# ScalarE instead of POOL makes the reciprocal deviation and shift of a layernorm, in a one-core macaron block with a selective scan

## The reference, cut to what matters

```python
def _layernorm(x, axis=-1, eps=1e-05):
    m = jnp.mean(x, axis=axis, keepdims=True)
    v = jnp.var(x, axis=axis, keepdims=True)
    return (x - m) / jnp.sqrt(v + eps)
...
    x = x + 0.5 * _L0_ffn_ref(_layernorm(x, axis=-1), L0_ffn_Ws, ...)
    x = x + _L0_attn_ref(_layernorm(x, axis=-1), ...)
    x = x + 0.5 * _L0_ffn_ref(_layernorm(x, axis=-1), L0_ffn_Ws, ...)
```

## Time and profile before

| what | value |
|---|---|
| median of 3 runs | 4454.32 us (4450.94 to 4455.48) |
| the profiled execution | 4447.92 us, span 4446.2 us |
| PE busy, mean granted clock | 3866.4 us (87%), 0.955 |
| DVE busy | 3971.1 us (89%) |
| ACT busy | 3327.9 us (75%) |
| POOL busy | 3950.6 us (89%) |
| DMA | 434.67 MB, mean 98 GB/s |
| chain that ended last, shares of the span | PE 39%, DVE 24%, issue 15%, POOL 12%, ACT 9% |

### The profile page before, as it was taken

How to read it: one execution, slowest core, us unless ns; L and a number is a source line. 1 busy time by engine, 2 the same in 40 slices (tenths; PEclk the granted TensorE clock), 3 DMA queues, 4 the chain that set the end, 5 groups by cost and what they waited for, 6 DMA issues and landing times.

```text
span 4446.2 us, 50132 instructions
## 1 busy us (share of the span) xinstructions
PE 3866.4 (87%) x12736; PEld 1277.6 (29%) x12736; DVE 3971.1 (89%) x5441; ACT 3327.9 (75%) x4991; POOL 3950.6 (89%) x1740
## 2 busy tenths in 40 slices
PE   6786877999999999999999999999999999678868
PEld 2221222232323323332232333223232323122223
DVE  2669999999999999999999999999999999999963
ACT  4567777877878787877878787887878777677744
POOL 0559999999999999999999999999999999999950
PEclk9898888999999999999999999999999999799979
DMA  2234554445444543444454445444544454434410
GB/s 77 60 81 99 115 117 97 96 108 117 94 98 112 112 96 92 116 108 102 96 116 100 97 101 122 96 102 103 117 94 95 113 116 94 112 95 111 94 34 5
DMA packets 151917, 434.67 MB, mean 98 GB/s; under 512 B 16402, under 2 KB 50451, under 8 KB 151124
## 3 DMA queue, kind: packets, MB, share of 16 engines
q1 hardware_dynamic: 151636, 431.46, 41.9%
HBM read 150.38 MB, written 12.58 MB: 37 GB/s over the span
## 4 chain that ended last, share of the span: by engine, by line
PE 39%; DVE 24%; issue 15%; POOL 12%; ACT 9%; DMA 1%; SPq 0%; DVEq 0%; ACTq 0%; POOLq 0%
DVE work L778 10%; POOL work L962 6%; PE d_ps L487 6%; POOL work L953 5%; PE s_ps L534 4%; DVE dA_ps L778 4%; PE y_ps L449 4%; PE b_ps L480 4%; PE a_ps L466 4%; DVE work L783 3%; PE a_ps L480 3%; PE s_ps L567 2%; DVE sg_sb L858 2%; PE b_ps L466 2%; ACT L637 2%
## 5 line engine op out<-in xcount | busy, mean ns | idle before, releaser
L962 POOL TENSOR_TENSOR work<-dd_sb,bc_sb 128x2048 f32<-128x2048 f32 x512 | 2327.9, 4547 | 49.3 <-DMA dd_sb<-dd_src 49.3
L609 ACT ACTIVATE dA_ps<-dd_sb,a_sb 128x512 f32<-128x512 f32 x2048 | 1367.3, 684 | 554.6 <-DVE work L783 290.1
L953 POOL TENSOR_TENSOR work<-work,bc_sb 128x1024 f32<-128x1024 f32 x640 | 1511.3, 2368 | 46.9 <-DVE work L778 46.5
L778 DVE TENSOR_TENSOR_SCAN work<-dA_ps,work 128x512 f32<-128x512 f32 x1280 | 1495.0, 1205 | 51.8 <-POOL work L962 41.4
L778 DVE TENSOR_TENSOR_SCAN dA_ps<-dA_ps,work 128x512 f32<-128x512 f32 x768 | 935.0, 1217 | 6.3 <-ACT dA_ps L609 4.8
L487 PE MATMUL d_ps<-sg_sb,wd_sb 128*128 128x512 f32 x1408 | 648.4, 593 | 4.8 <-DVE sg_sb L858 4.8
L449 PE MATMUL y_ps<-work,sel_sum 128*32 128x512 f32 x4096 | 578.2, 636 | 83.2 <-POOL work L953 56.3
L783 DVE TENSOR_TENSOR work<-dA_ps,bc_sb 128x512 f32<-128x512 f32 x768 | 523.2, 681 | 8.1
L466 PE MATMUL a_ps<-xT_sb,wg_sb 128*128 128x512 f32 x768 | 427.9, 640 | 113.0 <-ACT sg_sb L637 103.1
L466 PE MATMUL b_ps<-xT_sb,wg_sb 128*128 128x512 f32 x640 | 358.3, 642 | 59.0 <-DVE xs_sb L851 55.2
L637 ACT ACT_TABLE_LOAD x256 | 328.4, 1283 | 70.7 <-PE d_ps L487 66.5
(11 more groups left out here) (122 smaller groups left out, 4059.1 us busy)
## 6 DMA issues: line engine op xcount, KB each, us to landing
dd_sb<-dd_src SPq DMA_DIRECT2D x512, 512.0 KB, 8.5
bc_sb<-bc_rows SPq DMA_DIRECT2D x256, 512.0 KB, 5.3
xr_sb<-in_L_attn_x SPq DMA_DIRECT2D x16, 256.0 KB, 3.1
x<-xr_sb SPq DMA_DIRECT2D x16, 256.0 KB, 6.9
bc_rows<-dbc_sb SPq DMA_DIRECT2D x128, 32.0 KB, 1.7
xr_sb<-x SPq DMA_DIRECT2D x16, 256.0 KB, 2.9
out<-xr_sb SPq DMA_DIRECT2D x16, 256.0 KB, 6.9
wg_sb<-in_L_ffn_Wg SPq DMA_DIRECT2D x1, 1408.0 KB, 7.1
```

The source lines that it names most:

```text
L609: act.activation(dA_ps[:, g % NDA, :], dd_sb[:, b, c, 0, :], ACT.Exp, scale=a_sb[:, l, b, j, c:c + 1]).then_inc(dA_ready, 1)
L778: dve.tensor_tensor_scan(dA if on_dve(i) else tile, dA, tile, 0.0, ALU.mult, ALU.add).then_inc(scanned, 1)
L953: pool.tensor_tensor(work[:, g % RING], work[:, g % RING], bc_sb[:, j, 0, :].unsqueeze(1).broadcast_to([128, 2, T]), ALU.mult).then_inc(po ...
L962: pool.tensor_tensor(work[:, g % RING:g % RING + 2].rearrange("p h c t -> p (h c) t"), dd_sb[:, b, :, 1, :], bc_sb[:, j, 1, :].unsqueeze(1 ...
```

## The change

The four small POOL instructions of a norm go. In their place ACT runs seven: logarithm of the variance plus epsilon and the negated mean (`log_act`), exponential of -0.5 times the logarithm (`rstd_act`), and for each of the four row blocks the negated mean times that (`shift_act`). `bn_sb`, `mv_sb` and `rs_sb` get two halves that norms use in turn, so that DVE waits for the norm before the last (`nb_ready`, m - 1) and not for the last one. The unused `neg_half` and its memset on DVE go (`VPREP` 9 to 8), and so do `end_pool` and the POOL semaphores. PE's wait for the expert weights follows its table. All tables of numbers are set anew; two of them are shown.

```diff
-CORE = {"exp": -10, "scan": -1, "dbu": -12, "dve_prod": 1, "pool_prod": 12, "sum": 30, "y0": 88, "y1": 8}
+CORE = {"exp": -9, "scan": -1, "dbu": -34, "dve_prod": 2, "pool_prod": -15, "sum": 24, "y0": 87, "y1": 8}
-END = {"yt": 27, "xo": 33, "bn": 47, "nb": 60, "xtok": 67, "ht": 89, "h": 76, "store": 90, "acc": 4}
+END = {"yt": 19, "xo": 35, "bn": 36, "ln": 38, "rs": 47, "nb": 51, "xtok": 59, "ht": 77, "h": 77, "store": 90, "acc": 2}
...
-        bn_sb = sb("bn_sb", [128, TB, 6])
-        mv_sb = sb("mv_sb", [128, TB, 2])
-        rs_sb = sb("rs_sb", [128, 4, TB])
+        bn_sb = sb("bn_sb", [128, 2, TB, 6])
+        mv_sb = sb("mv_sb", [128, 2, TB, 2])
+        rs_sb = sb("rs_sb", [128, 2, 3, TB])
...
-                if t == FFN[0][0]:
+                if t == FFN[0][0] + min(0, *FFN_AT.values()):
                     pe.wait_ge(w_ffn, 16 * FFN_LOADS)
...
-                                          scale=rs_sb[:, 0, k:k + 1], bias=rs_sb[:, 2, k:k + 1])
+                                          scale=rs_sb[:, m % 2, 0, k:k + 1], bias=rs_sb[:, m % 2, 2, k:k + 1])
...
+            def log_act(what, f):
+                m = NORM_OF[what, f]
+                act.wait_ge(mv_done, m + 1)
+                if m > 1:
+                    act.wait_ge(xtok_ready, m - 1)
+                act.activation(rs_sb[:, m % 2, 0, :], mv_sb[:, m % 2, :, 1], ACT.Ln, bias=eps_sb[:, 0:1])
+                act.activation(rs_sb[:, m % 2, 1, :], mv_sb[:, m % 2, :, 0], ACT.Copy, scale=-1.0).then_inc(var_log, 1)
+
+            def rstd_act(what, f):
+                m = NORM_OF[what, f]
+                act.wait_ge(var_log, m + 1)
+                act.activation(rs_sb[:, m % 2, 0, :], rs_sb[:, m % 2, 0, :], ACT.Exp, scale=-0.5).then_inc(rstd_done, 1)
+
+            def shift_act(what, f):
+                m = NORM_OF[what, f]
+                act.wait_ge(rstd_done, m + 1)
+                for k in range(TB):
+                    last = act.activation(rs_sb[:, m % 2, 2, k:k + 1], rs_sb[:, m % 2, 1, k:k + 1], ACT.Copy,
+                                          scale=rs_sb[:, m % 2, 0, k:k + 1])
+                last.then_inc(nb_ready, 1)
...
-                if m > 0:
-                    dve.wait_ge(shift_done, m)
+                if m > 1:
+                    dve.wait_ge(nb_ready, m - 1)
...
-            def norm_pool(what, f):
-                m = NORM_OF[what, f]
-                pool.wait_ge(mv_done, m + 1)
-                if m > 0:
-                    pool.wait_ge(xtok_ready, m)
-                pool.tensor_scalar(rs_sb[:, 3, :], mv_sb[:, :, 1], EPS, None, ALU.add).then_inc(ve_done, 1)
-                pool.wait_ge(ve_done, m + 1)
-                pool.tensor_tensor(rs_sb[:, 0, :], rs_sb[:, 3, :], neg_half[:, :], ALU.pow).then_inc(rstd_done, 1)
-                pool.wait_ge(rstd_done, m + 1)
-                pool.tensor_tensor(rs_sb[:, 1, :], mv_sb[:, :, 0], rs_sb[:, 0, :], ALU.mult).then_inc(shift_done, 1)
-                pool.wait_ge(shift_done, m + 1)
-                pool.tensor_scalar(rs_sb[:, 2, :], rs_sb[:, 1, :], -1.0, None, ALU.mult).then_inc(nb_ready, 1)
```

More of the change, by code:

```diff
@@ L31 @@
 W, PERIOD = 128, 32
-CORE = {"exp": -10, "scan": -1, "dbu": -12, "dve_prod": 1, "pool_prod": 12, "sum": 30, "y0": 88, "y1": 8}
-PREP = {"dc1": 83, "dc0": 60, "sq": -20, "ms": -6, "rms": -10, "xn": -4, "xp0": 17, "conv0": 16, "xp1": 25, "conv1": 23,
-        "silu_xc": 27, "z0": 105, "zc0": 97, "z1": 114, "zc1": 106, "silu_z": 123, "wx": 46, "dbc": 38, "rows": 32, "dt0": 48,
-        "sp0": 52, "delta0": 57, "du0": 60, "dt1": 77, "sp1": 71, "delta1": 76, "du1": 79, "dd0": 63, "dd1": 135, "bc": 98}
@@ new lines @@
+PREP = {"dc1": 84, "dc0": 62, "sq": -14, "ms": -19, "rms": -6, "xn": -4, "xp0": 9, "conv0": 18, "xp1": 13, "conv1": 23,
+        "silu_xc": 27, "z0": 94, "zc0": 97, "z1": 106, "zc1": 105, "silu_z": 123, "wx": 29, "dbc": 46, "rows": 78, "dt0": 41,
+        "sp0": 49, "delta0": 61, "du0": 65, "dt1": 63, "sp1": 70, "delta1": 77, "du1": 79, "dd0": 56, "dd1": 178, "bc": 123}
+NEAR = {"dc1": 95, "dc0": 80, "sq": 16, "ms": 13, "rms": 24, "xn": 30, "xp0": 40, "conv0": 49, "xp1": 44, "conv1": 56,
+        "silu_xc": 59, "z0": 99, "zc0": 101, "z1": 105, "zc1": 108, "silu_z": 123, "wx": 65, "dbc": 60, "rows": 73, "dt0": 69,
+        "sp0": 73, "delta0": 81, "du0": 81, "dt1": 83, "sp1": 90, "delta1": 91, "du1": 92, "dd0": 86, "dd1": 174, "bc": 103}
@@ new lines @@
+POST = {"x1": 49, "wblk": 83, "h": 90, "attn": 90, "x2": 98}
+POST_NEAR = {"x1": -81, "wblk": 9, "h": 14, "attn": 20, "x2": 55}
+FFN_AT = {"gb": -2, "xs": 4, "g0": -8, "g1": 3, "g2": 5, "burst": 5, "u0": 7, "u1": 7, "u2": 18, "hh0": 13, "hh1": 14,
+          "hh2": 23, "down": 21}
+START = {"load": -96, "bn": -56, "ln": -52, "rs": -49, "nb": -46, "xtok": -45, "xt": -42, "xT": -40, "lg": -41, "lg_sb": -34, "mx": -32,
+         "mi": -30, "gap": -56, "we": -31, "eq": -24, "den": -56, "inv": -26, "comb": -49, "ct": -15, "gates": -20}
@@ L340, in build @@
         APREP = 2 + 2 * NL + NL * NBLK
-        VPREP, PPREP = 9, 10
+        VPREP, PPREP = 8, 10
         ps_of = {"a": a_ps, "b": b_ps}
@@ L648, in norm_act @@
                     last = act.activation(xtok[:, k, :], xr_sb[:, x_slot(FFN[f][1], n), k, :], ACT.Identity,
-                                          scale=rs_sb[:, 0, k:k + 1], bias=rs_sb[:, 2, k:k + 1])
+                                          scale=rs_sb[:, m % 2, 0, k:k + 1], bias=rs_sb[:, m % 2, 2, k:k + 1])
                 last.then_inc(xtok_ready, 1)
-            def start_act(t):
+            def log_act(what, f):
[16 more added lines that the diff above has]
+                last.then_inc(nb_ready, 1)
+            def start_act(t):
+                if (f := UNIT_OF.get(t - START["ln"])) is not None:
+                    log_act("start", f)
+                if (f := UNIT_OF.get(t - START["rs"])) is not None:
+                    rstd_act("start", f)
+                if (f := UNIT_OF.get(t - START["nb"])) is not None:
+                    shift_act("start", f)
                 if (f := UNIT_OF.get(t - START["xtok"])) is not None:
@@ L669, in end_act @@
             def end_act(t):
+                if (f := UNIT_OF.get(t - E * PERIOD - END["ln"])) is not None and FFN[f][1] == 1:
+                    log_act("ln2", f)
+                if (f := UNIT_OF.get(t - E * PERIOD - END["rs"])) is not None and FFN[f][1] == 1:
+                    rstd_act("ln2", f)
+                if (f := UNIT_OF.get(t - E * PERIOD - END["nb"])) is not None and FFN[f][1] == 1:
+                    shift_act("ln2", f)
                 if (f := UNIT_OF.get(t - E * PERIOD - END["acc"])) is not None:
@@ L865, in norm_dve @@
                 for k in range(TB):
-                    last = dve.bn_stats(bn_sb[:, k, :], xr_sb[:, x_slot(FFN[f][1], n), k, :])
+                    last = dve.bn_stats(bn_sb[:, m % 2, k, :], xr_sb[:, x_slot(FFN[f][1], n), k, :])
                 last.then_inc(bn_done, 1)
                 dve.wait_ge(bn_done, m + 1)
-                if m > 0:
-                    dve.wait_ge(shift_done, m)
+                if m > 1:
+                    dve.wait_ge(nb_ready, m - 1)
                 for k in range(TB):
-                    last = dve.bn_aggr(mv_sb[:, k, :], bn_sb[:, k, :])
+                    last = dve.bn_aggr(mv_sb[:, m % 2, k, :], bn_sb[:, m % 2, k, :])
                 last.then_inc(mv_done, 1)
@@ L1036, in _ @@
                 start_pool(t)
-                end_pool(t)
 def laid_out(name, a):
```

13 lines of the change are left out of this document (3 added, 10 removed).

## The result

The changed kernel takes 4473.37 us (median of 6 runs, 4470.05 to 4475.26), the kernel before 4452.63 us beside it (6 runs, 4446.46 to 4455.48). The ratio is 1.0048, 95% interval 1.0036 to 1.0061: **slower by about 0.5%**, where 4431 us was forecast. The profiled execution took 4474.74 us (span 4473.0), 26.8 us more than that of before.

The account below looks back on a forecast made before the run. DVE was taken to bound the middle and POOL the full stretches at the ends. The terms -10.0 - 8.2 + 6 - 7 - 4 = -23 us, applied to the median 4454.32 us, gave 4431 us, range 4392 to 4462.

Parts of the forecast that it names:

- The view of the middle: 1075 to 3575 us: DVE sets the pace at 96.2% busy; POOL, nearly as full at 96.5%, keeps up.
- (c): Ahead of a unit: ACT's added norm steps are covered by PE, price 0; otherwise up to 1.2 us a norm.
- (d): After a first unit: ACT's norm steps ahead of `dc1` make `xs` on DVE late, 0.5 us a round, +6 us.
- (f): `attn` moved ahead of the second `g`: `x2` waits less, the silu's burst may be held; booked 0, -1.8 to +2.0 a round.
- (h): Last phases: `dd_sb` loads together on SP, ahead of `bc_sb`, save part of POOL's 7.3 us wait, -4 us.
- (b): Stretches at the ends where POOL is full: all 2.04 us of each of four norms count, -8.2 us.
- (a): In the middle: DVE's wait for POOL's product, 8.3 us, comes back; -10.0 us over the 3000 us alike.
- The price of the norm on ACT: Seven small instructions added on ACT take 1.2 us a norm, 58 us in all, within ACT's idle time.
- (e): `sp0` ahead of an exponential fills ACT's wait for a scan; the burst begins 0.6 us earlier a round, -7 us.
- The third rival: ACT's steps ahead of `dc1` and a burst held by `attn` keep exponentials from DVE: +18 us, 4472 us, chance 0.13.

Follow-up runs that it names:

- e1: The changed code with the old order tables, so only the norm moves from POOL to ACT: 4468.83 us, 1.0044 to the kernel before.
- e2: The old code with the new order tables, the norm left on POOL between its old neighbours: 4515.94 us, 1.0152 to the kernel before.
- e9: The changed kernel with the norm's rows after a first unit put back behind `dc1` on ACT: 4458.84 us, 1.0018 to the kernel before.
- e5: The changed kernel with the next expert's first silu input `g0` ahead of the router's product on PE: 4462.87 us, 1.0030 to the kernel before.
- e10: The changed kernel with the edits of e5 and e9 together: 4451.11 us, 1.0005 to the kernel before.
- e4: The changed kernel with `attn` on PE back behind the `u` products and `x2` back behind two `hh` and a scan: 4490.21 us, 1.0092.

## Why the prediction was wrong, by its steps

The view of the middle was right in its main part: DVE sets the pace, and POOL's time comes back only as idle time of POOL (its busy time fell by 81 us in all, 82 were foreseen; table loads 541 again). The step that failed first is one that the sum never names: every term of the middle, (c), (d) and (f) above all, takes PE to deliver at the pace that it had before. The middle was booked at -10.0 + 6 - 7 = -11 us and cost +21 in nine of its twelve rounds, 18 of them in rounds where PE's clock falls behind `attn`. Beside it (h) failed, (c) had the wrong reason, (d) was too small, and (b) is not shown.

- **What was missing: PE's clock.** The earlier trace rows showed 0.99 in the middle, and I took PE as the same engine before and after. It falls at places where PE works on small matmuls or waits (11 times in the nine rounds of before, 21 times now); the change moved behind these places products that DVE needs at once. In the changed kernel the rounds with a fall behind `attn` are 3.1 us longer, and that makes 18 of 21 us in the nine rounds.
- **(a) held as a wait, not as time.** DVE no longer waits for POOL in the middle, neither here nor in e1, where the norm alone moved. But other waits came in its place, and at full clock a round is no shorter.
- **(b) is not shown.** Phases 4 to 8 take 244.6 us instead of 247.7, 3.1 of the 4.1 us for two norms. But with the norm alone off POOL (e1) they take 248.2, and with the new orders and the norm still on POOL (e2) 246.5: POOL's time by itself gave nothing there. At the end nothing came at all: POOL is still busy 122.4 of 125 us.
- **The price of the norm on ACT held.** The seven instructions' own times are 8.7 + 5.7 + 5.8 + 25.2 us for 30 norms, 1.51 us each, but neighbours overlap, and what they take from ACT is the time to the start of its next instruction: 0.29 us for lines 656 and 657, 0.10 for 662 and 0.87 for 668 in the norm below, 1.26 in all, where 1.2 was booked. The estimate from the Trainium skill, page "ScalarE: Activation LUTs", section "What ACT_TABLE_LOAD costs", was 1.41 us; the trace agrees with it in the time in which at least one of the seven runs, 0.38 + 0.19 + 0.84 = 1.41 us here.

```profile
L668 ACT ACTIVATE rs_sb<-rs_sb 128x1 f32<-128x1 f32 x120 | 25.2, 281 | 0.0
...
L656 ACT ACTIVATE rs_sb<-mv_sb,eps_sb 128x4 f32<-128x4 f32 x30 | 8.7, 291 | 0.1
...
L662 ACT ACTIVATE rs_sb<-rs_sb 128x4 f32<-128x4 f32 x30 | 5.8, 192 | 0.0
L657 ACT ACTIVATE rs_sb<-mv_sb 128x4 f32<-128x4 f32 x30 | 5.7, 191 | 0.0
```

```profile
2116.39 0.29 ACT L656 ACTIVATE rs_sb<-mv_sb,eps_sb 128x4 f32<-128x4 f32 x1
2116.58 0.19 ACT L657 ACTIVATE rs_sb<-mv_sb 128x4 f32<-128x4 f32 x1
2116.68 0.68 ACT L608 ACTIVATE dA_ps<-dd_sb,a_sb 128x512 f32<-128x512 f32 x1
2117.29 0.19 ACT L662 ACTIVATE rs_sb<-rs_sb 128x4 f32<-128x4 f32 x1
2117.39 0.67 ACT L608 ACTIVATE dA_ps<-dd_sb,a_sb 128x512 f32<-128x512 f32 x1
2118.00 0.84 ACT L668 ACTIVATE rs_sb<-rs_sb 128x1 f32<-128x1 f32 x4
2118.87 1.65 ACT L647 ACTIVATE xtok<-xr_sb,rs_sb 128x128 f32<-128x128 f32 x4
```

- **(c) failed as an argument.** "Covered by PE, price 0" looked at the rows and at PE, not at the copies behind the rows on ACT. With the old orders (e1) it costs: `lg_sb` 37.5 us for 24.1. With the new orders, which have `zc1` ahead of the next exponential, the price is 0 again as far as `lg_sb` shows it (14.2).
- **(d) had the right mechanism and too small a size.** 0.5 us a round were booked, 0.77 measured at `xs`; with what hangs on it, the clock included (e9), the place is worth 13 us, not 6.
- **(e) came out in size, and its reason is not shown.** `hh`'s waits for the first `u` in `b_ps` (5.6 us in ten rounds) are no longer among DVE's, the 0.6 us a round that were booked. But in e5 and e10, with `sp0` at the same place, they are 11.5 and 8.9 us, so what stands on PE ahead of `u` decides them, too.
- **(f) came out inside its bounds, for another reason than weighed.** `x2` gains 1.2 us a round and `lg_sb` 1.0; the 1.2 us that `hh` loses come with the half clock (1.4 to 2.0 us at it, 0.33 without), not from the silu that `attn` passed. Putting `attn` back (e4) is worse.
- **(h) failed, and by the orders.** The seven phases from 3789 us (before) to the last phase's start take 445.9 us instead of 439.9. With the old orders and the norm on ACT (e1) they take 438.5, with the new orders and the norm on POOL (e2) 448.1. The waits of POOL that were to shrink from 7.3 us are about 16, four in each kernel; the trace does not name what ended them (first e2, then the changed kernel):

```profile
POOL work L962 <- issue: 15.2, 4, 5.1
```

```profile
POOL work L993 <- issue: 16.9, 4, 5.1
```

The third rival (ACT late, 4472 us) has the time nearly to the microsecond, by luck: it has one of its two places (`xs`, 0.77 where it had 1.0) and nothing of the clock. The other, a burst held by `attn`, is not what happened, and DVE's wait for ACT at the scans is no more than 5.0 us in the middle (2.0 before).

Left open: why the clock falls behind the first router product in nine rounds of ten now and in two before, though PE's order and its waits of 0.78 and 0.28 us there are the same; and whether `attn` in pieces would help.

## What to carry to other kernels

Moving work off an engine that is full pays only if the engine that sets the pace waits for it; here 98 us of POOL work bought nothing that shows, even with two places of the change mended (e10, 1.0005), and the place where the work lands decides the sign. On an engine in order, look at what stands behind the new instructions and which shared bank it frees (`dc1`, the gate copy, `x2`), not only at those instructions. And where rounds of one execution with the same order differ by more than the gain you hope for, read PE's granted clock round by round before you read the waits.
